# A selective-scan pipeline in which GpSimd scales its half of dBu after the product with C

## What is computed

```
dA  = exp(delta[..., None] * A)
dBu = delta[..., None] * Bm[:, :, None, :] * u[..., None]
def step(h, xs):
    dA_t, dBu_t, C_t = xs
    h = dA_t * h + dBu_t
    y = jnp.einsum('ben,bn->be', h, C_t)
    return (h, y)
```

## Time and profile before

| | us |
|---|---|
| median of 3 runs | 4126.22 |
| lowest, highest | 4122.41, 4132.3 |
| the profiled execution | 4136.71 |
| its span | 4135.0 |

### The profile page before, as it was taken

The page is one execution under the profiler, slowest core; times in us unless marked ns, Lnnn a source line. Parts: engine busy times, 40 slices in busy tenths (PEclk is TensorE's granted clock), DMA queues, the critical chain, the costliest instruction groups (busy, mean ns, idle before and its releaser), DMA issues. The chain is left out here.

```text
span 4135.0 us, 67083 instructions
## 1 busy us (share of the span) xinstructions
PE 3497.5 (85%) x22974; PEld 2989.5 (72%) x22974; DVE 2836.2 (69%) x3589; ACT 2941.1 (71%) x6612; POOL 2830.2 (68%) x3087
## 2 busy tenths in 40 slices
PE   4677778998989898989989898989899898886776
PEld 2456667787878787878878787878788787764555
DVE  1466778787877777787878777777778686844321
ACT  1568777887878787878878787878787887835122
POOL 0378888786868686878878686868788787823100
PEclk8799999999999999999999899999999999977666
DMA  3112222222222222222122222222221222201000
GB/s 153 45 50 76 63 76 62 79 62 72 62 74 63 71 64 68 67 58 81 55 79 64 70 63 71 65 68 66 64 72 57 77 65 67 64 20 38 14 7 3
DMA packets 140897, 258.00 MB, mean 62 GB/s; under 512 B 15905, under 2 KB 33313, under 8 KB 140081
## 3 DMA queue, kind: packets, MB, share of 16 engines
q1 hardware_dynamic: 140482, 252.95, 20.3%
HBM read 233.16 MB, written 5.05 MB: 58 GB/s over the span
## 5 line engine op out<-in xcount | busy, mean ns | idle before, releaser
L656 POOL TENSOR_TENSOR g<-hst,c_bc 128x512 f32<-128x512 f32 x1536 | 1988.2, 1295 | 433.5 <-PE ps_y L558 359.9
L638 DVE TENSOR_TENSOR_SCAN hst<-decay,ps_b 128x512 f32<-128x512 f32 x1536 | 1831.4, 1211 | 603.1 <-PE ps_b L530 424.6
L599 ACT ACTIVATE decay<-delta,acoef 128x256 f32<-128x256 f32 x3072 | 1378.2, 499 | 4.4 <-DVE hst L638 4.2
L618 POOL TENSOR_TENSOR dbut<-dut,bcm 128x256 f32<-128x256 f32 x1536 | 952.4, 621 | 578.1 <-remote 348.4
L530 PE MATMUL ps_b<-ident,dbut 128*128 128x128 f32 x6144 | 990.1, 287 | 362.9 <-ACT dbut L609 203.4
L530 PEld LDWEIGHTS ps_b<-ident,dbut 128*128 128x128 f32 x6144 | 746.9, 148 | 446.6 <-ACT dbut L609 349.2
L558 PE MATMUL ps_y<-ident,g 128*128 128x128 f32 x6144 | 949.4, 279 | 5.8 <-POOL g L656 4.8
L558 PEld LDWEIGHTS ps_y<-ident,g 128*128 128x128 f32 x6144 | 756.1, 145 | 115.1 <-issue 37.8
L609 ACT ACTIVATE dbut<-dut,bcm 128x256 f32<-128x256 f32 x1536 | 767.1, 500 | 25.1 <-PE ps_b L530 21.7
L1261 PEld LDWEIGHTS ps_x<-v,pT 128*128 128x128 f32 x2048 | 277.0, 213 | 15.4 <-issue 11.4
L1261 PE MATMUL ps_x<-v,pT 128*128 128x17 f32 x2048 | 277.2, 274 | 3.1 <-ACT pT L1297 2.3
(11 more groups left out here) (188 smaller groups left out, 4186.6 us busy)
## 6 DMA issues: line engine op xcount, KB each, us to landing
c_bc<-c_rows SPq DMA_DIRECT2D x768, 256.0 KB, 3.2
rows_bc<-mod_rows SPq DMA_DIRECT2D x16, 384.0 KB, 4.2
weights<-in_weights_dram SPq DMA_DIRECT2D x1, 5792.0 KB
ada_w<-in_ada_w_dram SPq DMA_DIRECT2D x1, 5120.0 KB
x<-in_x_dram SPq DMA_DIRECT2D x16, 256.0 KB, 4.0
x0p<-x SPq DMA_DIRECT2D x16, 256.0 KB, 2.3
xr<-x SPq DMA_DIRECT2D x16, 256.0 KB, 3.7
x<-x SPq DMA_DIRECT2D x16, 256.0 KB, 2.3
```

Source lines behind the costliest of these rows:

```text
L599: last = nc.scalar.activation(decay[:, u % (DA_AHEAD + 2), e, :], delta[s][:, eb, :], ACT.Exp, scale=acoef[:, s, eb, n:n + 1])
L618: nc.gpsimd.tensor_tensor(dbut[:, u % NDBU, 1, :], dut[s][:, 1, hh * HALF * P:(hh + 1) * HALF * P], bcm[s][:, 1, n:n + 1].broadcast_to([P, ...
L638: nc.vector.tensor_tensor_scan(line(hst[:, u % NHST, :, :].rearrange("p e t -> p (e t)")), line(decay[:, u % (DA_AHEAD + 2), :, :].rearran ...
L656: nc.gpsimd.tensor_tensor(g[:, u % NG, :, :], hst[:, u % NHST, :, :], c_bc[:, k % NCB * CHUNK + n % CHUNK, :].unsqueeze(1) .broadcast_to([ ...
```

## The change

In the loop over the units GpSimd's call of `scale_p(u + 3)` moves from before the product with C of unit u to behind it.

```
@@ -646,8 +646,6 @@
                 for u in range(self.units):
                     n = u % N
                     k = u // CHUNK
-                    if u + P_AHEAD < self.units:
-                        self.scale_p(pool, u + P_AHEAD)
                     if u % CHUNK == 0:
                         pool.wait_ge(S[f"c_in_{k % NCB}"], 16 * (k // NCB + 1))
                     pool.wait_ge(S["scan_done"], u + 1)
@@ -656,6 +654,8 @@
                     nc.gpsimd.tensor_tensor(g[:, u % NG, :, :], hst[:, u % NHST, :, :],
                                             c_bc[:, k % NCB * CHUNK + n % CHUNK, :].unsqueeze(1)
                                             .broadcast_to([P, HALF, T]), ALU.mult).then_inc(S["g_ready"], 1)
+                    if u + P_AHEAD < self.units:
+                        self.scale_p(pool, u + P_AHEAD)
                 pool.wait_ge(S["y_taken"], self.groups(self.units))
                 pool.wait_ge(S["g_used"], self.units)
```

## The result

The changed kernel takes **4583.89 us** (median of 4 runs, 4551.41 to 4592.95) against 4129.26 us for the kernel before on the same occasion: a ratio of **1.108, 95% interval 1.105 to 1.111**, or 455 us more. The prediction was 4514, with a range of 4390 to 4640. The profiled execution is the quickest of the four, 4551.41 us with a granted clock of 0.907; its span is 414.7 us over that of before. The other three had clocks of 0.896 to 0.900.

The account below looks back on a forecast made before the run. It took TensorE, near saturation in full passes, as the bound. New waits summed 12 x 28 + 22 + 12 + 15 + 3 = 388 us, added to 4126 for 4514, with a range of 4390 to 4640.

Parts of the forecast that it names:

- the loop of one position: TensorE's sum frees g, GpSimd multiplies by C, scales a half, TensorE transposes: 2.73 us, one position of TensorE work between.
- Y(v-6): TensorE's four matmuls summing unit v-6's product with C; they release the g buffer for unit v-3's product.
- empty position: Place in TensorE's order with little or no other layers' work; there it would stand still up to 1.41 us.
- The sum for a full pass: 34 charged positions in a 96-unit pass, 35 us; growth 25 to 35 after absorption by idle time, 28 taken.
- t: Other layers' TensorE work at a unit's position; each charged wait was 1.41 us less this.
- Other passes: Growth outside the 12 alike passes: last full one 22 us, two thinner 12 and 15, 64- and 32-unit together 3.
- the clock: TensorE's granted clock falling in idler passes: 2% of 190 us, 4 us a pass, 50 in all; outside the sum.
- more than the sum: Rival: all idle time stays beside the new waits and the granted clock falls, +500 to +600 us; chance 0.08.
- the main case: TensorE's new waits for GpSimd's half add up, partly absorbed by idle time: +300 to +500 us, chance 0.74.
- Same time: Rival: GpSimd's half is still in time, ScalarE's half being the later one; 4126 us, chance 0.05.
- faster: Rival: at pass starts the product with C no longer queues behind the scaling; 4116 us, chance 0.03.
- half absorbed: Rival: hidden TensorE waits shrink and give time back; +50 to +260 us, 4180 to 4385, chance 0.10.

Follow-up runs that it names:

- the control run: The changed kernel with three C buffers instead of four and nothing else: 4606.67 us, ratio 1.1148 to the kernel before.
- the first time: The changed kernel with four g buffers instead of three and three C buffers instead of four: 4165.73 us; the order of before with these buffers took 4110.95.
- the second: The changed kernel with GpSimd's half two units ahead instead of three, four g buffers and three C buffers: 4790.93 us, ratio 1.1594 to the kernel before.

## Why the prediction was right, and where it was off

**The mechanism held.** The alternation is the same with each half one slot later, and the loop of one position closes: in 386 of the 434 waits the product ahead of the late half had waited for Y(v-6). Its length was put at 2.73 us from three rows of different stretches, and 2.72 is the median of the 434. At unit 27 the prediction had B wait 1.42 us; the profile records 1.25 us, and the start is 1.84 us after Y(22), where 0.44 was usual: 1.40 more. The second empty position adds as much again: B(30) starts 6.97 us after B(27), where it was 5.56, 1.41 more. The recorded idle time is smaller by 0.17 because the modelled end of the last matmul before a wait lies that much behind the start of a next one that doesn't wait.

**The sum for a full pass held.** It charged 34 places with 35 us, less what existing idle time absorbs. Measured were 434 / 12 = 36 waits a pass with 28.6 us of recorded idle time, and 36 x 0.17 = 6.1 for what the recording hides: 34.7 us. The split held as well: all 21 positions with t under 0.25 us wait in each of the 12 passes, 23.0 us a pass recorded and 26.6 with what is hidden, for the 26.4 that were charged to 19 of them. Waits for the scan fell from 56 to 20 us over the 12 passes, so 3.0 a pass were absorbed, as the prediction said that some would be. From B(4) to B(95) the 12 full passes grew by 29.9 us on average; the prediction took 28. (34.7 less 3.0 is 31.7; the other 1.8 us are not explained.) The 28 was a choice between 25 and 35 and not a result of rows, so that it came this close is in part luck.

**Other passes.** The last full one grew by 20.6 us (predicted 22), the two thin ones by 13.5 and 10.6 (12 and 15), the short ones by 5.3 and 1.7 together with the same measure (3). The sum of all is 410 us against a span that grew by 414.7, and against 388 predicted. The gaps between passes stayed.

**The term that was mis-sized is the clock.** I had it as a rival with 50 us and left it out of the sum. In the profiled execution it did nothing, since the full passes were granted 0.92 to 0.97, around the 0.96 of before, and that run came to 4551, 26 over the 4525 predicted for it; 22 of these are the passes above (410 for 388). The three others took 25 to 42 us more with clocks of 0.896 to 0.900 where this one had 0.907, and the control run's profiled execution, of the same order, took 4636.81 at 0.886. That is about 40 us for 0.01 of clock. So of the 67 us between 388 and the 455 of the medians some 27 are in the growth of the profiled run (415), and some 40 go with the clock of the others, which were not profiled. Each of the four runs lies in the range.

The reason given for that rival doesn't hold for waits of this size. It took from three of the earlier trace rows that a pass with more idle time is granted less. The fourth row there has the lowest clock, 0.92, with TensorE 91% busy, and in the changed kernel the two thin passes, busy for only 70% and 77%, were granted 0.95 and 0.99, more than before. The other half of "more than the sum" fell too: the idle time of before was partly absorbed, as the main case had it.

**The rule of the Trainium skill** ("Perfetto Trace Analysis", the section on the GPSIMD engine instruction) is that a GpSimd span is unreliable and that the spacing of starts is to be used. The trace bears it out here: the loop's measured 2.72 us agrees with the value read from starts and one end (2.73), not with the sum of two durations (2.77).

**What I said the profile would show.** GpSimd's wait for Y growing from 25.2 us a pass to about 50: it is 51.1 in the pass at 2302 us.

```profile
POOL g L654 <- PE ps_y L558: 51.1, 53, 4.4
...
PE ps_b L530 <- issue: 14.7, 20, 1.2
PE ps_b L530 <- ACT dbut L609: 12.4, 13, 1.3
...
PE ps_b L530 <- POOL dbut L618: 3.4, 3, 1.8
```

The full pass between 229 and 239 us: 230.4 to 241.7 in the profiled run. TensorE's share about 84%: 197.71 of 230.5 is 86%. But the first sign failed as I had put it. TensorE's wait for GpSimd's dbut should have grown from 37.9 us to over 300, and the profile gives 42.7 in the whole program. By my own criterion ("under 100 us: the loop reading is wrong") I would have thrown out a right reading. The waits are there, 343 us in the 12 passes, under ScalarE's name and under "issue". The criterion should have been the times themselves: the end of P(v) beside the start of B(v).

**The rivals.** Same time, faster and half absorbed fell with the result; the first also with the pairing above.

## What to carry to other kernels

"Three units ahead" in a loop says little. What counts is which product stands ahead of the step in its engine's list, what that product waits for, and how many positions of the waiting engine's list lie between that release and the use. Here a buffer of g bought back most of a lost unit of lead, all but 55 us of it the first time and 184 the second: a loop through a buffer's release costs nothing while the other engine has more work inside it than the loop is long, and an empty position is paid in full as soon as it has not, or in part where its neighbour has paid (at position 10 the wait was 1.24 us on average, at 11 behind it 0.74). When an engine is nearly always busy, as TensorE was here at 95%, look for such a loop before moving anything on its neighbours, and charge it position by position, not by the mean; a waiting engine's releaser is to be confirmed by pairing units, since the name beside an idle time can be that of another unit's instruction.

## What the runs showed of the hardware that was not expected

- TensorE's granted clock fell to 0.60 in the passes where it waited some 2 us before each unit's transposes and was busy for 337.18 of 532.10 us, and the transposes' steps went from 0.44 to between 0.9 and 1.0 us. With waits of 0.1 to 1.3 us at 36 of 92 units (the changed kernel) it stayed between 0.92 and 0.97 in the full passes. These are mean values between the two levels, 1.2 and 2.4 GHz.
- The clock differs between passes of one execution that hold the same work and the same idle time: in the changed kernel 0.97 in the pass at 2302 us and 0.92 in the one at 2806, 230.5 and 241.7 us. The four runs of the changed kernel spread over 41 us in the same way, while the runs of the kernel before stayed within some 25 us. So a difference of 20 to 40 us between kernels with such waits should not be read as a mechanism.
- The recorded spans of two GpSimd instructions that follow each other without a wait overlap by about 0.05 us (2361.05 + 1.28 = 2362.33, the next starts at 2362.28).
